# Masked relative products stored by tile, head and query instead of query pair, tile and head

## The reference

```python
idx = clip(arange(S)[None, :] - arange(S)[:, None], -64, 64) + 64      # [q, k]
rk, rv = embK[idx], embV[idx]
logits = einsum('bhqd,bhkd->bhqk', q, k) + einsum('bhqd,qkd->bhqk', q, rk)
w = softmax(logits)
out = einsum('bhqk,bhkd->bhqd', w, v) + einsum('bhqk,qkd->bhqd', w, rv)
out = out @ Wo.T + bo
x = x + layernorm(attention(layernorm(x)))
x = x + layernorm(layernorm(x) @ (ternary(weight) * alpha).T + bias)
```

## Time and profile before

| what | us |
|---|---|
| runs, not profiled | 2827.56 median (2824.03, 2827.56, 2828.02) |
| profiled execution, its own time | 2825.32 |
| its span in the trace | 2823.5 |
| granted TensorE clock over the span, as a share of full speed | 0.981 |
| PE, DVE, ACT, POOL busy | 2627.9, 2035.1, 1558.8, 955.3 |

### The profile page before, as it was taken

How to read it: one execution, slowest core, us unless ns; L and a number is a source line. 1 busy time by engine, 2 the same in 40 slices (tenths; PEclk the granted TensorE clock), 3 DMA queues, 4 the chain that set the end, 5 groups by cost and what they waited for, 6 DMA issues and landing times.

```text
span 2823.5 us, 102954 instructions
## 1 busy us (share of the span) xinstructions
PE 2627.9 (93%) x43410; PEld 1977.3 (70%) x43410; DVE 2035.1 (72%) x5187; ACT 1558.8 (55%) x2993; POOL 955.3 (34%) x2275
## 2 busy tenths in 40 slices
PE   5899999999999999999999999999999999999995
PEld 4577777677776777767776777767777677777773
DVE  4776678676786778866788667876678766787774
ACT  2455556455555555555555565545565455565651
POOL 3113333433334323343234332334323433331026
PEclk8799999999999999999999999999999999999997
DMA  7556654456454564555645556446654456445410
GB/s 220 173 136 177 174 150 125 128 153 186 123 152 131 160 166 135 134 149 156 172 119 147 164 153 168 118 124 176 167 143 126 115 174 187 137 131 144 133 44 27
DMA packets 605048, 409.11 MB, mean 145 GB/s; under 512 B 149162, under 2 KB 604330, under 8 KB 604330
## 3 DMA queue, kind: packets, MB, share of 16 engines
q1 hardware_dynamic: 604586, 402.54, 50.7%
HBM read 206.84 MB, written 194.90 MB: 142 GB/s over the span
## 4 chain that ended last, share of the span: by engine, by line
PE 69%; DVE 16%; issue 5%; ACT 4%; POOL 3%; SPq 2%; DMA 1%; DVEq 0%; ACTq 0%; POOLq 0%
PE oacc L797 15%; PE logitsT L759 15%; PE scores L736 14%; PE logitsT L764 7%; DVE maxes L1016 6%; DVE junk L1013 5%; PE misc L860 4%; PE misc L693 4%; PE misc L822 3%; PE misc L834 2%; PE misc L710 2%; PE misc L810 2%; ACT wxr L1216 2%; POOL rs L1249 1%; PE misc L720 1%
## 5 line engine op out<-in xcount | busy, mean ns | idle before, releaser
L1013 DVE CUSTOM_DVE_ANT_1 junk<-scores,bands 128x512 bf16<-128x512 f32 x988 | 679.7, 688 | 594.4 <-PE scores L736 575.4
L759 PE MATMUL logitsT<-qs,ks 98*128 98x128 bf16 (+3 forms) x9088 | 995.2, 216 | 32.2 <-ACT wxr L1216 23.3
L1216 ACT ACTIVATE wxr<-logitsT 128x512 f32<-128x512 f32 x1024 | 601.9, 602 | 568.2 <-PE logitsT L759 471.4
L759 PEld LDWEIGHTS logitsT<-qs,ks 98*128 98x128 bf16 (+1 forms) x9088 | 679.6, 99 | 256.5 <-issue 95.9
L1216 ACT ACTIVATE wy<-logitsT 128x512 f32<-128x512 f32 x1024 | 587.2, 597 | 437.6 <-PE logitsT L759 427.0
L736 PE MATMUL scores<-ks,qs 101*128 101x256 bf16 (+10 forms) x4096 | 719.1, 291 | 78.5 <-DVE maxes L1016 39.0
L1016 DVE TENSOR_REDUCE maxes<-scores 128x1 f32<-128x512 f32 x1024 | 701.5, 685 | 2.3 <-PE scores L736 2.3
L736 PEld LDWEIGHTS scores<-ks,qs 96*128 96x128 bf16 (+3 forms) x4096 | 299.0, 99 | 265.2 <-DVE maxes L1016 120.1
L764 PE MATMUL logitsT<-ident,bands 128*128 128x128 f32 x2048 | 468.0, 280 | 0.0
L1244 POOL TENSOR_SCALAR rs<-rs 128x1 int32<-128x1 int32 (+1 forms) x224 | 48.3, 216 | 995.5 <-DVE rs L924 992.9
L764 PEld LDWEIGHTS logitsT<-ident,bands 128*128 128x128 f32 x2048 | 292.5, 143 | 33.4 <-issue 0.6
(11 more groups left out here) (136 smaller groups left out, 2587.0 us busy)
## 6 DMA issues: line engine op xcount, KB each, us to landing
bs<-praw SPq DMA_DIRECT2D x256, 512.0 KB, 4.3
bands<-bs SPq DMA_DIRECT2D x224, 512.0 KB, 4.4
ks<-kd SPq DMA_DIRECT2D x64, 384.0 KB, 5.0
qs<-qd SPq DMA_DIRECT2D x112, 192.0 KB
bands<-bs SPq DMA_DIRECT2D x128, 128.0 KB, 3.8
qd<-qparts SPq DMA_DIRECT2D x64, 192.0 KB, 3.2
kd<-kparts SPq DMA_DIRECT2D x64, 192.0 KB, 2.6
qd<-qparts SPq DMA_DIRECT2D x64, 128.0 KB, 2.6
```

Of the source, the lines that this page charges most:

```text
L759: mm = e.matmul(lt[:, c * P + q0:c * P + q1], kk[0:depth, h, kt * P:(kt + 1) * P], qs[i][0:depth, h, q0:q1], start=q0 == 0, stop=not near, ...
L1013: e.tensor_tensor_reduce(junk[:], scores[:, 0:512].rearrange("p (a c) -> p a c", a=2), banded, 1.0, LOWEST, ALU.add, ALU.max, mx[:, h, 0:1 ...
L1216: e.activation(dst, src, ACT.Exp).then_inc(exp_ready, 1)
```

## The change

`relout` gets the order tile, head, pair, query instead of pair, tile, head, query. The masked product reads the same numbers from PSUM and the same mask in the same order, and stores each pair of numbers at its new place, 128 bytes after the one before. The matmuls of `relative_sum` read, for each of the four tiles, 32 numbers in a row, and then go on 1 KB further. The scratch use before the loop reads and writes 64 numbers in a row as before. Instructions, their number, their order on each engine and their waits are the same on all engines.

```diff
-        relout = sb("relout", [P, 16, QUAD, HG, 2])
+        relout = sb("relout", [P, QUAD, HG, 16, 2])
...
                             mm = e.matmul(mt[32 * j:32 * j + 32, :, 32 * jq:32 * jq + 32], relsel[:, jq, :],
-                                          relout[:, :, :, 4 * blk + j, :].rearrange("p i t c -> p t i c"), start=jq == 0,
+                                          relout[:, :, 4 * blk + j].rearrange("p t i c -> p t (i c)"), start=jq == 0,
                                           stop=True, skip_group_check=True)
...
-                    bt_h = relout[0:SPLIT, 0].rearrange("p t h c -> p (t h c)").bitcast(BF16)
+                    bt_h = relout[0:SPLIT, 0, 0:2].rearrange("p h i c -> p (h i c)").bitcast(BF16)
...
-                    e.tensor_tensor(relout[:, 8 * part:8 * part + 8].rearrange("p i t h c -> p (i t h) c"),
-                                    m[:].rearrange("p (a c) -> p a c", c=2),
-                                    relmask[:].rearrange("p (a c) -> p a c", a=1).broadcast_to([P, 256, 2]),
+                    e.tensor_tensor(relout[:, :, :, 8 * part:8 * part + 8, :].rearrange("p t h i c -> p i (t h) c"),
+                                    m[:].rearrange("p (i a c) -> p i a c", i=8, c=2),
+                                    relmask[:].rearrange("p (i a c) -> p i a c", i=1, a=1).broadcast_to([P, 8, QUAD * HG, 2]),
                                     ALU.mult).then_inc(rel_ready, 1)
```

## The result

The changed kernel takes 2809.57 us, the median of six runs (2807.2 to 2812.81), against 2827.02 for the kernel before in runs beside it (2824.03 to 2830.15). The ratio is 0.9939, with a 95% interval of 0.9927 to 0.9952: faster by 17.4 us, of which the interval allows 13.6 to 20.6. The forecast was 2815, with a range of 2809 to 2829.

The account below looks back on a forecast made before the run. PE was taken to bound the kernel, with nearly all of L822 on its path. 13.0 us saved x 0.95 = 12.4; 2825.32 - 12.4 = 2812.9, plus 2.2 for the median of runs: 2815, range 2809 to 2829.

Parts of the forecast that it names:

- What bounds the kernel: PE, busy 93% of the span; nearly all of L822, 3% of the chain, was taken to lie on the path.
- the mechanism: Faster reads at L822, blocks of 1.08 to 1.17 us: 2812.7 to 2818.6 us, chance 0.66.
- The size of a block: L822's 16 matmuls, now 1.30 to 1.35 us, were to take 1.10 to 1.12 us, saving 13.0 us.
- the one on the 32 stationary columns: At L822, 12 ns of load paid once (block 1.08 us) or at each of eight groups of records (1.17 us).
- The correction from L810: L810's excess of 3.9 ns a record, beside L822's 7.0, left 0.8 ns a record that doesn't grow with columns.
- The warning that L810's pairs lie at another distance: L810's pairs lie 1 KB apart and L822's 256 bytes, so the reasoning from L810 was called weaker than it looks.
- The rival that named "four strips that read `relout` at once": No saving: 32 stationary columns or four strips at once set L822's pace, not pairs; 2827 or 2824 us, chance 0.20.
- The sentence that dismissed a collision: Four reads 128 bytes apart could meet in memory, but L797's four, 1 or 2 KB apart, keep 1.07 us.
- Pass-through: 5% of L822's 13.0 us let go where PE meets a DVE or ACT result not yet waiting, leaving 12.4 us.
- The store: L1047, the DVE's masked product storing pairs 128 bytes apart, was to stay at 680 ns.
- The slow-store rival: Each number stored at L1047 takes three turns or more, L1047 at 1.74 us: 2850 us, chance 0.09.
- Its formula: Extra time x for each L1047 costs 2x - 0.24 us in each of 14 quads, x - 0.56 in 18, where positive.

Follow-up runs that it names:

- the padded run: Changed kernel with 16 bytes of padding behind each head's 1 KB in wxr, so L810's pairs lie 1040 bytes apart, not 1024: 2807.88 us, ratio to before 0.9937.

## Why the prediction was right, and where it was not

**What bounds the kernel.** Right. The chain gave L822 3%, as much as its whole busy time, and 15.0 us of busy time became 17.4 us of time. The 2.4 us beyond are not explained. In the two profiled executions the span fell by 17.0 us: 15.0 in L822, 1.3 in the busy time of PE's other lines and 0.7 in its idle time. The rest lies within the interval, and kernels with the same blocks spread over 5 us.

**The number.** 2809.57 us lies 3.1 us below the span from 2812.7 to 2818.6 us that the mechanism gave. It is within the range only because the low end was put at 2809 for the scatter of single runs, 0.6 us below what was measured. That much is luck.

**The size of a block.** 1.08 us was one end of the forecast and 1.11 its middle. The step that was mis-sized is the one on the 32 stationary columns: the 12 ns for their load are paid at the first records alone (298 ns) and the median record is at 273. The correction from L810 pulled the wrong way. It split L810's excess into a part by columns and a fixed part, and took both for properties of pairs; the padded run shows that 2.7 of its 3.9 ns a record went with 16 bytes of padding ((690 - 224) / 31 = 15.0, against 17.7), and nothing here shows the fixed part. The warning that L810's pairs lie at another distance was the right one, and distance turned out to be the point.

**The reason.** Half wrong. The forecast said that a strip pays for pairs. It pays only while the other strips read in its way: 2.48 against 2.46 us one strip after another, and 1.09 to 1.15 us for pairs in other places, against 1.32. The rival that named "four strips that read `relout` at once" had the mechanism and drew the wrong conclusion from it, that the change would then save nothing. The sentence that dismissed a collision because L797's strips lie 1 or 2 KB apart and keep their pace compared streams that read in a row with streams that step by 256 bytes; the changed kernel, whose strips lie 128 bytes apart and read in a row, keeps that pace too.

**The rule on lines of 16 bytes.** The rival took from the Trainium skill, "Advanced Engine Details and Errata", section "Memory Cachelines", that two hits on a line are enough for full performance. This case agrees for a strip alone (109 ns a record with pairs as with rows), for runs of four numbers (1.08 us), and for the DVE's store of pairs (681 ns). It doesn't for four strips that read pairs at once 256 bytes apart, 1.32 us against 1.08.

**Pass-through.** 5% was let go for nothing: 15.0 us of L822 brought all of 15 and more. With 13.0 x 0.95 = 12.4 the sum was short of the measured 17.4 by 2 us of block size, 0.6 of pass-through and 2.4 unexplained.

**The store.** Right for pairs. The slow-store rival had its price right in kind: with single numbers L1047 took 1058 ns, an extra of 0.38 us. Its formula gives 14 x (2 x 0.38 - 0.24) = 7.3 us and nothing in the other quads, and PE's idle time did grow by 7.3 us; the other runs spread over 4.5, so the agreement is no closer than that. Two readings under it are slightly off, and the first would raise it: when PE waits for the masked product, L822 starts 1473.78 - 1472.69 - 1.04 = 0.05 us after its end, so of the 0.24 us only 0.19 were slack; and between the two products the DVE idles for 0.10 us in each of the 14 quads, a gap too short to be marked in the timeline. It was also said to become dangerous at 1.24 us, which no run reached.

## What to carry to other kernels

Matmuls of several strips that run at once can hinder each other where their moving operands are read. Where each read pairs in steps of 256 bytes, the bytes between the strips decided: 1.39 us with 8 of them, 1.09 with 64. Smaller steps, a read in runs of 16 bytes, or 16 bytes of padding on a step of 1024 took most or all of the cost away. The engine that writes the tensor did not notice a store in pairs (681 ns against 680), but it did notice single numbers (1058). Before such a saving is counted, look at who idles behind it: at L822 the other engine waited for 2.6 us and all of the 15.0 us came through; at L810 it was mostly busy, and of 13.7 us the time shows 1.7, no more than scatter.

## What the runs showed of the hardware

- A float32 matmul in a strip of 32 columns that reads pairs 256 bytes apart is as fast alone as one that reads in a row: its records of 128 columns start 109 ns apart in both. With four such strips at once, 8 bytes apart, they start 137 ns apart, and the block of 16 matmuls is 22% longer (1.32 and 1.08 us); with rows the four keep 109 ns.
- The same four strips, 64 bytes apart: 1.09 us. Steps of 32, 64 and 128 bytes with strips 8 bytes apart: 1.11 to 1.15 us. Single numbers 128 bytes apart, strips 4 bytes apart: 2.20 and 2.29 us.
- The DVE stores pairs of float32 128 bytes apart at the pace of a row (681 ns for 512 numbers), and single numbers at 1058 ns.
- Four strips that read pairs 1024 bytes apart, 128 bytes from each other: 16 bytes of padding on the step took a block of 32 records with 64 moving columns from 0.78 to 0.69 us.
